# Delta stage: the third long product of a slot stands in front of the state product in every slot

## What is computed

```python
def kda_scan(q, k, v, g, beta):
    def step(S, inp):
        qt, kt, vt, gt, bt = inp
        S = S * jnp.exp(gt)[..., None]
        vd = (vt - jnp.einsum('bhkv,bhk->bhv', S, kt)) * bt[..., None]
        S = S + kt[..., None] * vd[:, :, None, :]
        return (S, jnp.einsum('bhkv,bhk->bhv', S, qt))
    ...
q, k, v = (causal_conv_silu(x @ W) for each)     # 16 heads of 128
g = -exp(A_log) * softplus(x @ Wfa @ Wfb + dt_bias)
beta = sigmoid(x @ Wb)
o = kda_scan(l2norm(q) * SCALE, l2norm(k), v, g, beta)
o = o * rsqrt(mean(o * o) + EPS) * o_norm_w * sigmoid(x @ Wga @ Wgb)
x = x + o @ Wo
```

## Time and profile before

| what | value |
|---|---|
| median of 3 runs | 3643.24 us (3642.28 to 3643.34) |
| the profiled execution, its own time | 3644.98 us |
| its span, first to last instruction | 3642.8 us |
| mean granted TensorE clock | 0.972 |
| PE busy | 3432.4 us (94%) |
| DVE busy | 1945.9 us (53%) |
| ACT busy | 1429.7 us (39%) |
| POOL busy | 125.0 us (3%) |

### The profile page before, as it was taken

How to read it: one execution, slowest core, us unless ns; L and a number is a source line. 1 busy time by engine, 2 the same in 40 slices (tenths; PEclk the granted TensorE clock), 3 DMA queues, 4 the chain that set the end, 5 groups by cost and what they waited for, 6 DMA issues and landing times. The chain is left out here.

```text
span 3642.8 us, 85340 instructions
## 1 busy us (share of the span) xinstructions
PE 3432.4 (94%) x37232; PEld 1644.3 (45%) x37232; DVE 1945.9 (53%) x3346; ACT 1429.7 (39%) x3321; POOL 125.0 (3%) x457
## 2 busy tenths in 40 slices
PE   7989999996789999999999999999999869999999
PEld 4444444443344444444445444444544434444444
DVE  2221111113787888789877978888898531111111
ACT  2020000003457656765665576566656531000000
POOL 0000000000000000000000000000000000000000
PEclk9999999998989999999999999999999969999999
DMA  4020100004101111121011211111211033101000
GB/s 165 0 95 0 29 29 0 12 0 152 34 25 34 49 51 38 39 66 41 29 64 38 63 34 46 43 38 40 66 39 36 11 133 95 29 0 29 0 12 12
DMA packets 83725, 156.21 MB, mean 43 GB/s; under 512 B 8782, under 2 KB 33998, under 8 KB 79516
## 3 DMA queue, kind: packets, MB, share of 16 engines
q1 hardware_dynamic: 83356, 150.77, 12.7%
HBM read 133.71 MB, written 17.04 MB: 41 GB/s over the span
## 5 line engine op out<-in xcount | busy, mean ns | idle before, releaser
L1366 PE MATMUL psum<-dl_xt,dl_wqkv 128*128 128x512 f32 x1536 | 777.5, 623 | 11.7 <-DVE dl_qkv L1010 11.7
L541 DVE SCALAR_TENSOR_TENSOR f_act_g<-psum,f_bup,f_act_g 128x512 f32<-128x512 f32 x96 | 72.0, 750 | 930.0 <-ACT f_act_g L495 930.0
L1010 DVE SCALAR_TENSOR_TENSOR dl_qkv<-psum,dl_par,dl_qkv 128x511 f32<-128x511 f32 (+2 forms) x576 | 430.7, 748 | 14.2 <-DVE dl_qkv L1017 0.2
L495 ACT ACTIVATE f_act_g<-psum,f_bgate 128x512 f32<-128x512 f32 x96 | 66.0, 687 | 923.1 <-PE psum L432 923.1
L1366 PEld LDWEIGHTS psum<-dl_xt,dl_wqkv 128*128 128x128 f32 x1536 | 257.5, 189 | 251.2 <-issue 211.8
L432 PE MATMUL psum<-xnt_sb,wup 128*128 128x512 f32 x768 | 345.2, 592 | 0.0
L428 PE MATMUL psum<-xnt_sb,wgate 128*128 128x512 f32 x768 | 345.2, 592 | 0.0
L450 PE MATMUL psum<-f_wdown,f_hidden 128*128 128x512 f32 x768 | 344.9, 592 | 0.0
L1373 PE MATMUL psum<-dl_wo,dl_sg 128*128 128x512 f32 x512 | 261.0, 624 | 3.2 <-DVE dl_qkv L1010 2.8
L428 PEld LDWEIGHTS psum<-xnt_sb,wgate 128*128 128x128 f32 x768 | 145.9, 190 | 183.7 <-issue 183.7
L450 PEld LDWEIGHTS psum<-f_wdown,f_hidden 128*128 128x128 f32 x768 | 145.9, 190 | 183.7 <-issue 183.7
(11 more groups left out here) (200 smaller groups left out, 4535.0 us busy)
## 6 DMA issues: line engine op xcount, KB each, us to landing
dl_wqkv<-in_dw_qkv SPq DMA_DIRECT2D x192, 256.0 KB, 2.6
dl_wo<-in_dwo SPq DMA_DIRECT2D x16, 1024.0 KB, 5.6
f_weights_b<-f_weights_by_expert SPq DMA_DIRECT2D x48, 256.0 KB, 6.4
wgate<-in_wgate SPq DMA_DIRECT2D x2, 3072.0 KB, 19.4
wup<-in_wup SPq DMA_DIRECT2D x2, 3072.0 KB, 24.6
f_wdown<-in_wdown SPq DMA_DIRECT2D x2, 3072.0 KB, 12.3
x_sb<-in_x SPq DMA_DIRECT2D x4, 1024.0 KB, 9.0
x_after_experts<-x_sb SPq DMA_DIRECT2D x16, 256.0 KB, 2.0
```

Of the source, the lines that this page charges most:

```text
L1010: tap_ = lambda dl: dve.scalar_tensor_tensor(y_[:, dl:TT], ps[:, bank, 0:TT - dl], par[:, h, 4 * a + 3 - dl:4 * a + 4 - dl], y_[:, dl:TT], ...
L1366: last = pe.matmul(ps[:, bank, :], wq[:, n % RING, m, :], xt[:, u // HG % 2, m, :], start=(m == 0), stop=(m == KC - 1))
```

## The change

The list of slots with a short job at `inner` is no longer asked for. Before, product 2 of the long job stood in front of the state product only where nothing stood at `inner`, and behind it otherwise. Now it stands in front in every slot that has a long job, behind the `inner` jobs.

```diff
@@ -1476,7 +1476,6 @@
                         job = main_job(k, sl)
                         previous = (k - 1, SLOTS - 1) if sl == 0 else (k, sl - 1)
                         put_out = 0 <= previous[0] < UNITS
-                        filler = short_jobs(k, sl, "inner")
                         if run:
                             keys_state(k, sl)
                         if put_out:
@@ -1490,12 +1489,10 @@
                         if run:
                             solve_u(k, sl)
                         all_short(k, sl, "inner")
-                        if job and not filler:
+                        if job:
                             long_job(job, (2,))
                         if run:
                             state_step(k, sl)
-                        if job and filler:
-                            long_job(job, (2,))
                         all_short(k, sl, "split")
                         if job:
                             long_job(job, (3,))
```

## The result

The changed kernel took 3697.68 us (median of 4 runs, 3692.68 to 3700.34), the kernel before in the same comparison 3642.88 us (4 runs, 3642.28 to 3643.34). The ratio is 1.0149, 95% interval 1.0131 to 1.0167. That is 54.8 us slower; the forecast was 52 us slower. The profiled execution of the changed kernel is the lowest of its four runs, 3692.68 us.

A forecast was written before the change was run, and what follows sets the result against it. PE sets the pace in most slots, with DVE or ACT setting it in three places. A, B and C sum to 3.64 us per full unit; with corrections +52 us on 3643.2 gives 3695 us, range 3678 to 3714.

The forecast's parts named there:

- Split pairs: On PE, parting two long products by a state product makes the slot 0.20 us longer, in 144 of the moves.
- The allowance for a cheaper switch behind L1381: Four slots per unit: switching behind L1381's rows could be up to 0.10 us cheaper, -5.6 us in all.
- A: Slot 12's solve to slot 1's: 1.85 us longer per full unit, four split pairs (0.79) and slot 0's lateness (1.06).
- B: Slot 1's solve to slot 6: 0.59 us longer per full unit, through slot 1's later addition, softplus and ACT's queue.
- the room: DVE's 0.46 us wait before slot 2's addition, taken from slot 1's 1.06 us lateness, leaving 0.59.
- the sign I offered to the reader: In the profile after, slot 3's state product would wait about 1.03 us for `ubuf`.
- C: Slot 6 to slot 12's solve: 1.2 us longer per full unit through DVE's work; about 0.4 in units 4 and 8.
- Rival 1: Faster: the waits for `ubuf` in slot 10 go and nothing follows, 7 us gained, 3636 us; chance 0.04.
- rival 2: No change: late additions are hidden, or split cost and slot 10's gain cancel; within 7 us, chance 0.03.
- rival 3: Only PE's own price is paid: 29 us less slot 10's 7 us, 3665 us; chance 0.05.
- Rival 4: The switch of form on PE is free, only the state product's lateness is paid: 3681 us; chance 0.08.
- Rival 5: The clock falls after PE's longer waits: 1.7 us per stretch, one per unit gives +24, 3719 us; chance 0.08.

The follow-up runs named there:

- E2: Kernel before with product 2 moved in front of the state product in slots 12 to 15 alone: 3656.78 us, ratio 1.0033.
- E1: Kernel before with product 2 moved in front of the state product in slot 0 alone: 3661.01 us, ratio 1.0044.
- E6: Kernel before without DVE's second softplus pass in slot 0: 3628.11 us, ratio 0.9959.
- E7: Changed kernel without DVE's second softplus pass in slot 0: 3687.24 us, ratio 1.0116 to the kernel before.
- E4: Kernel before with product 2 moved in front of the state product in slot 1 alone: 3653.97 us, ratio 1.0029.
- E5: Kernel before with product 2 moved in front of the state product in slot 10 alone: 3654.43 us, ratio 1.0032.
- E3: Kernel before with product 2 moved in front of the state product in slots 6 to 10 alone: 3672.38 us, ratio 1.0074.
- V1: Kernel before with slot 0's second filler (vrow) put behind the state product instead of in front: 3632.86 us, ratio 0.9972.
- V2: Kernel before with product 2 put behind the state product in slot 2: 3638.78 us, ratio 0.9987.
- V3: Kernel before with both V1's edit in slot 0 and V2's in slot 2: 3629.02 us, ratio 0.996.
- E8: Changed kernel run once more, unedited, for a second profile: 3700.45 us, ratio 1.0155 to the kernel before.

## Why the prediction was right, and where it was off

**The forecast** was 3695, 2.7 us under the median, and the mechanism is the one given: the price of a parted pair on PE, and a later state product wherever DVE's run behind it is unbroken. That the time came out so close is in part luck: the order itself costs 48.7 us in the trace after, 3 less than the sum of 52, and the median lies 5.0 us above the profiled execution for reasons that the sum didn't hold.

**Split pairs.** Forecast 0.20 for each, measured 0.197 (E2). The rule of the Trainium skill, "TensorE: Matmul & The Clock Gate", Part 2, by which the drain overlaps the next fill, would have made it nothing; E2 contradicts that for a neighbour of another form. (The prediction puts that rule at 13 us in one place and at 14 in another; its own terms, 14 x 1.0, give 14.) The allowance for a cheaper switch behind L1381 (-5.6 in the bounds) wasn't needed: slot 0 alone was 1.05 late, the full price.

**A: 1.85, measured 1.84.** Four pairs of 0.197 and 1.057 in slot 0. E1, E2 and the pair E6 and E7 show both parts by themselves. The wait of slot 1 is 1.66, to the hundredth of the forecast. One reading was wrong without consequence: DVE idles over 2 us in front of the additions of slots 13 to 15, but not of slot 12, where it is still at other work, and the addition starts 0.6 us after the state product's end. The keys product comes 2.7 us after it, so there was room all the same.

**B: 0.59, measured 0.51.** The mis-sized step is the room: I took only the 0.46 in front of slot 2's addition, but DVE's idle time between the two additions is 0.53 in all, which leaves 0.53 of the 1.06. From solve to solve the trace after has slot 1 +0.198, slot 2 +0.190 and slot 3 +0.122, and E4 the same within 0.003. Slot 2 has +0.19 for a reason that I hadn't counted. ACT's sigmoid of the gates is later and so is the PSUM bank that the gate product L1436 needs:

```profile
1662.90 0.60 ACT L885 ACTIVATE dl_sg<-psum 128x512 f32<-128x512 f32 x1 [3.87 <-DVE dl_kkt L1047]
```

That is ACT's timeline after, unit 5; L1436 starts at 1663.55, right behind it. Since PE arrives later at slot 3's state product, its wait there is 0.76 and not the 1.03 forecast. The 1.03 is 0.64 + 0.59 less slot 1's 0.20; slot 2's 0.19 came off as well, and in E4 too the wait grew by 0.12 only. It is an error in the sign I offered to the reader, not in the time, for `ubuf` sets it.

**C: 1.2, measured 1.05 to 1.20.** The chain was right (slots 7, 8 and 9 +0.20 each, slot 10 -0.26, slot 11 +0.83), and the wait of slot 12 of 2.03 is within 2.0 to 2.5. One step was off: slot 8's keys product didn't wait at all, so slot 9 began 0.40 late where I had 0.5. I gave units 4 and 8 about 0.4, where the trace shows 0.76 and 0.70. How much of that is the change can't be told from one trace, since the pause itself differs from run to run: in the runs that leave slots 6 to 10 alone and have no stretch there, C changes in these units by anything from -0.59 (E2, unit 8) to +0.15 (E6, unit 8). Unit 12 was full, as I had counted it: its 0.72 holds -0.43 in slot 6, and every other run, those included that don't touch this slot, has the same -0.43 there (-0.42 in E1 and E4). It is the profile of before that was longer in this one place.

**Rival 1** fell by E5, **rival 2** by E1 to E4, of which each alone is slower, **rival 3** by E1 against E6 and E7: 0.20 would be the price of PE alone in slot 0, 1.05 was paid. **Rival 4** fell by E2.

**Rival 5, the clock,** is where the prediction was weakest. I made it one case of +24 us with chance 0.08, or nothing. It came in part: one stretch in one profile, six in another, each mostly 1.6 us (I had 1.7). By my own words, falls inside units 1 to 14 were a sign of being wrong; the first profile has its one new fall in unit 0, but the second has five in units 4 to 9. The median, 5.0 us over the profiled execution with its one stretch, may hold some three of them more. That is not shown: the slower executions' mean granted clock, 0.971 or 0.972, is no lower than the 0.971 of the profiled one. That the waits before (0.80, and up to 1.4 in slot 12) brought no fall was read correctly, but waits of 1.66 and 2.03 us were outside what those rows could speak for. It would have been better as a term of its own, between 0 and 14 x 1.6 = 22 us, in the upper bound.

**What stays open.** The waits of some 2.0 us in slot 12 are alike in four profiles, the two of the changed kernel and those of E3 and E7, yet these have 1, 6, 8 and 9 stretches: only some of the waits are followed by half clock, and two executions of one program differ. Nothing run here shows what decides it. That the stretches go with the waits, and not with something else in those slots, is shown only so far: E2, E4, V1, V2 and E6, where the solves of slots 1 and 12 wait at most 1.45 us in units 1 to 13, had none; E5, with 1.90 in slot 12, had two, both behind such a wait; E1, with 1.66 in slot 1, had three, two of them behind it and one behind the pause in unit 8. V3 had one, behind the pause in unit 4. These two pauses are short, 1.48 us (E1) and 1.55 (V3), while one of 1.59 in V2 was followed by none, so the length alone doesn't decide it.

The pause of PE in units 4 and 8 has no releaser in the profile. In the traces of all runs, in each such pause over 1 us, PE starts again 1.21 to 1.61 us after a transfer of 16 KB on the DMA queue named `instruction` has ended. The pause is 1.44 us in unit 4 before, 2.07 after. It looks like PE waiting for the next piece of its program; that is argued from the times, and no run tests it.

## What to carry to other kernels

Price a moved instruction by the engine that waits for what stands behind it: take the run of that engine up to its next hand-over, subtract the idle time inside the run, and what is left is the cost, whatever the first engine gains. A wait that an edit removes is worth nothing before the next wait of the same engine has been checked (E5: 0.45 us gone, 0.62 more two slots on), and the same reasoning turned round found the faster order (V3, 0.4% under the kernel before). When variants of a few tenths of a per cent are compared, compare starts of like instructions unit by unit, since totals also hold stretches of lower clock that come in other numbers in each run; and where one unit differs, look whether it is the profile of before that is odd there, as in unit 12.

## What the runs showed of the hardware

- A pair of 128x512 float32 products parted by a state product of another shape costs 0.197 us more than one in a row, the same in slots 12 to 15 of units 0 to 13 (E2).
- Waits of PE of 1.66 to 2.1 us, with PE busy 42.87 of the 45.00 us ahead (the window of E8), were in some cases followed by 3.4 us of granted clock 0.50, 1.2 GHz; such a stretch made its unit mostly 1.6 us longer. The kernel before has none in units 1 to 13.
- The count isn't a property of the program: 1 and 6 in two executions of the changed kernel.
- PE's pauses without a releaser in units 4 and 8 ended 1.21 to 1.61 us after a 16-KB transfer on the `instruction` queue, in the traces of all runs.
